# An LSTM and six layers of windowed attention on one core: the layer stage's hardware loops written out

## The reference

```python
def step(carry, xw_t):                      # LSTM, 1024 steps in sequence
    a = xw_t + prev_h @ Wh
    i, f, o, g = sigmoid, sigmoid, sigmoid, tanh of the four parts of a
    next_c = f * prev_c + i * g
    next_h = o * tanh(next_c)
...
for i in range(6):
    x = attn_layer(shift_tokens(x), Wqkv[i], q_scale[i], k_scale[i], Wo[i]) + x   # 16 heads of 64, windows of 64 with one look back
    x = ffn_layer(shift_tokens(x), ln_g[i], ln_b[i], W1[i], b1[i], W2[i], b2[i]) + x
return x_in + x
```

## Time and profile before

| | |
|---|---|
| time, median of 3 runs | 5339.57 us (5339.14 to 5344.78) |
| the profiled execution | 5329.88 us |
| its span, first to last instruction | 5326.9 us |
| busy: TensorE, weight loads | 4817.3 us (90%), 3753.0 us (70%) |
| busy: VectorE, ScalarE, GpSimd | 3541.4, 2630.4, 1899.0 us |
| start of the first slot's scores, start of the last chunk's | 630.39 us, 4857.08 us |
| instructions in the trace | 206473 |

### The profile page before, as it was taken

The page is one execution under the profiler, slowest core; times in us unless marked ns, Lnnn a source line. Parts: engine busy times, 40 slices in busy tenths (PEclk is TensorE's granted clock), DMA queues, the critical chain, the costliest instruction groups (busy, mean ns, idle before and its releaser), DMA issues.

```text
span 5326.9 us, 206473 instructions
## 1 busy us (share of the span) xinstructions
PE 4817.3 (90%) x79632; PEld 3753.0 (70%) x79632; DVE 3541.4 (66%) x14167; ACT 2630.4 (49%) x8193; POOL 1899.0 (36%) x2070
## 2 busy tenths in 40 slices
PE   4665699999999999999999999999999999999888
PEld 1445577777777777777777777777777777776666
DVE  8665566676667667676666666676666666666554
ACT  0112355555555555555555555455455555455554
POOL 3640233333333333333333333333333333334442
PEclk6555699999999999999999999999999999999999
DMA  3020122322322322323322322332332332233431
GB/s 128 2 85 0 45 82 86 107 85 89 105 82 79 119 82 78 106 82 90 107 82 78 119 82 78 104 94 81 104 90 82 106 95 79 89 105 91 120 118 53
DMA packets 311470, 464.73 MB, mean 87 GB/s; under 512 B 213264, under 2 KB 239888, under 8 KB 297616
## 3 DMA queue, kind: packets, MB, share of 16 engines
q1 hardware_dynamic: 310544, 451.92, 28.3%
HBM read 381.93 MB, written 69.93 MB: 85 GB/s over the span
## 4 chain that ended last, share of the span: by engine, by line
PE 59%; issue 12%; DVE 9%; POOL 4%; ACT 3%; ACTq 0%; POOLq 0%; DMA 0%; DVEq 0%; SPq 0%
PE mm L914 12%; PE gates L185 12%; PE st L1026 7%; PE gates L177 5%; PE dd L1026 4%; PE st L953 3%; PE pt L1053 3%; PE pt L1061 3%; PE tt L926 2%; PE pt L967 2%; POOL va L817 2%; PE dd L983 2%; DVE pr L1398 2%; PE st L995 1%; PE st L943 1%
## 5 line engine op out<-in xcount | busy, mean ns | idle before, releaser
L802 POOL TENSOR_TENSOR turned<-raw,rotl 128x256 f32<-128x256 f32 x768 | 716.4, 948 | 1810.6 <-ACT raw L1145 1523.2
L914 PE MATMUL mm<-wqkv,xa 128*128 128x512 f32 x2304 | 1196.6, 632 | 11.1 <-DMA rot<-in_rotary 8.5
L185 PE MATMUL gates<-hp,whp 128*128 128x6 bf16 x28672 | 849.9, 166 | 23.7 <-DVE hp L230 23.4
L185 PEld LDWEIGHTS gates<-hp,whp 128*128 128x128 bf16 x28672 | 784.7, 96 | 59.0 <-DVE hp L230 31.9
L1196 ACT ACTIVATE pr<-st,nb,qn 128x128 f32<-128x128 f32 x1536 | 686.8, 462 | 134.4 <-DVE nb L1386 133.6
L192 ACT ACTIVATE state<-gsum 128x16 f32<-128x16 f32 x896 | 195.1, 218 | 987.2 <-DVE gsum L200 979.1
L914 PEld LDWEIGHTS mm<-wqkv,xa 128*128 128x128 f32 x2304 | 391.3, 196 | 249.3 <-issue 227.5
L177 PEld LDWEIGHTS gates<-hp,whp 128*128 128x128 bf16 x14336 | 425.7, 96 | 149.0 <-issue 91.0
L177 PE MATMUL gates<-hp,whp 128*128 128x2 bf16 x14336 | 485.7, 163 | 27.5 <-DVE hp L215 27.3
L200 DVE TENSOR_REDUCE gsum<-gates 128x16 f32<-128x48 f32 x896 | 182.0, 203 | 489.8 <-PE gates L185 483.2
L810 POOL TENSOR_TENSOR qn<-ss,power 128x8 f32<-128x8 f32 x192 | 321.1, 1672 | 514.5 <-DVE ss L1357 505.3
(11 more groups left out here) (135 smaller groups left out, 9796.9 us busy)
## 6 DMA issues: line engine op xcount, KB each, us to landing
wqkv<-in_Wqkv SPq DMA_DIRECT2D x288, 512.0 KB, 3.9
w<-in_W SPq DMA_DIRECT2D x48, 1364.0 KB, 5.8
wo<-in_Wo SPq DMA_DIRECT2D x48, 1024.0 KB, 5.5
w<-in_W SPq DMA_DIRECT2D x48, 768.0 KB, 4.5
kT<-k_windows SPq DMA_DIRECT2D x96, 256.0 KB, 5.2
va<-v_windows SPq DMA_DIRECT2D x96, 256.0 KB, 5.1
k_windows<-kT SPq DMA_DIRECT2D x96, 256.0 KB, 4.2
v_windows<-vb SPq DMA_DIRECT2D x96, 256.0 KB, 4.5
```

The source lines that it names most:

```text
L185: last = nc.tensor.matmul(g[:, m * PARTS * BATCH:(m + 1) * PARTS * BATCH], self.whp[:, p, k, m * P:(m + 1) * P], self.hp[:, k, :, :].rearr ...
L802: ins = nc.gpsimd.tensor_tensor(dst[:, :, a, :], src[:, :, 1 - a, :], tab[:, :, a, :].broadcast_to([P, 8, HALF]), ALU.mult)
L914: ins = nc.tensor.matmul(mm[c % 2][:, :], shifted(xa, y.b, k), wqkv[:, c, k, :], start=(k == 1), stop=(k == 0))
```

## The change

The `Fori` loops over chunks and layers in the layer stage become Python loops, on all five engines. All 96 slots are written out one after the other in each engine's stream. `c`, `l`, `it` and the step numbers are then Python numbers: every wait compares with a constant and every address is fixed. The order of the instructions in a slot isn't changed. The loop of the first stage stays.

```diff
@@ passes(): TensorE, VectorE, ScalarE, GpSimd
-            with eng.Fori(0, CHUNKS - 1) as c:
-                with eng.Fori(0, DEPTH - 1) as l:
-                    layer(c, l, l + c * DEPTH, True)
-                last_layer(c, c * DEPTH + (DEPTH - 1), True)
-            c = CHUNKS - 1
-            with eng.Fori(0, DEPTH - 1) as l:
-                layer(c, l, l + c * DEPTH, False)
-            last_layer(c, c * DEPTH + (DEPTH - 1), False)
+            for c in range(CHUNKS):
+                recur = c < CHUNKS - 1
+                for l in range(DEPTH - 1):
+                    layer(c, l, c * DEPTH + l, recur)
+                last_layer(c, c * DEPTH + (DEPTH - 1), recur)
```

## The result

The changed kernel takes 5176.9 us in the median of 4 runs (5173.6 to 5177.4), the kernel before 5339.4 us beside it (5329.1 to 5344.8). The ratio is 0.9697, with a 95% interval of 0.968 to 0.9713. The forecast was 5138 us with a range up to 5172; the time is 39 us above the one and 5 us above the other. The profiled execution took 5177.4 us, its span is 5175.6 us.

The account below looks back on a forecast made before the run. TensorE and VectorE waiting for code after taken loop jumps was taken as the bound. Savings of 180 + 21 + 1 = 202 us took the profiled 5329.9 to 5128; with 9.7 carried, 5138 us, range 5097 to 5172.

Parts of the forecast that it names:

- the jumps' missing code: Layer stage: TensorE and VectorE wait for code after 34 taken loop jumps; removing them saves 180 us after corrections.
- The base of the sum: Recurrent layer stage without jumps: 7 chunks x (10 x 48.43 + 47.17 + 45.66) = 4040 us, against 4226.7 in the trace.
- The last chunk: Slots without recurrence: removing jumps saves nothing there, removing registers 0.1 x 10 = 1 us.
- granted clock 1.00 from slot 1 to the end: Sign of being right: TensorE's clock stays full through all slots after the first.
- registers, 0.25 us per slot: Loop waits and addresses become constants in the layer stage: 0.25 us for 84 slots, 21 us saved; range 0 to 0.75.
- the correction for `k` = 0, 5 us: Slots of the first kind may be 0.15 us longer than slot 9; times 35, 5 us less gain.
- the excess behind a jump as "two things": Slots just behind a jump take 50.77 us through VectorE's late start and TensorE's half clock for 4.8 us.
- 9.7 us from the profiled execution to the median: Median of the runs lay 9.7 us over the profiled execution before; carried, it turns 5128 into 5138 us.
- Registers at 1 us per slot: Rival, chance 0.09: register instructions beside the recurrence's waits cost 1 us per slot, giving 5075 us.
- Only the gap goes, 5216: Rival, chance 0.06: only the 3.0 us gap at each of 34 jumps goes, 102 us, with registers 22: 5216 us.
- the trace speaks against the Trainium skill: VectorE's loop body would fit the skill's 512 held instructions, yet 4.6 us pass behind its jump.
- Code streamed as a cost: Rival, chance 0.03: ScalarE, GpSimd and SyncE must fetch straight code, 4.6 us once per slot, 440 us: 5580 us.

Follow-up runs that it names:

- pe_dve: Changed kernel with only TensorE's and VectorE's streams written out, loops and registers kept on the other three engines: 5186.0 us, 0.972 of the kernel before.
- pe_only: Changed kernel with only TensorE's stream written out, loops and registers kept on the other four engines: 5377.9 us, 1.0073 of the kernel before.
- dve_only: Changed kernel with only VectorE's stream written out, loops kept on the other engines: 5328.3 us, 0.9989 of the kernel before.
- fill_end: Changed kernel plus two useless 448-column matmuls per slot, placed near the slot's end: 5179.5 us, 0.9712 of the kernel before.
- fill_mid: Changed kernel plus two useless 448-column matmuls per slot, placed in the second recurrence step: 5212.7 us, 0.9777 of the kernel before.
- pad: Changed kernel with W2's last, 42-row block multiplied with all 128 rows, `u` cleared once: 5076.6 us, 0.9521 of the kernel before.
- before_pad: Kernel before, loops kept, with W2's last, 42-row block multiplied with all 128 rows: 5307.1 us, 0.9948 of the kernel before.
- reg: Changed kernel with a zero register added to `it` and step number, so waits and `hist` addresses are computed in registers: 5188.7 us, 0.9719 of the kernel before.
- pad_reg: Changed kernel with full-height W2 matmuls, plus a zero register added to `it` and step number on every engine: 5086.5 us, 0.9534 of the kernel before.

## Why the prediction missed by 39 us

**Right: the jumps' missing code.** That TensorE's 34 late starts and the half clock behind them would go, worth 5.5 us a jump, is shown by the waits and by pe_dve, which gains nearly all of it, where pe_only and dve_only gain nothing. The base of the sum, slots without a jump, held in form: 48.38 measured for 48.43, 47.07 for 47.17, 45.55 for 45.66 us. The last chunk gave what the registers gave, 38.62 for 38.72. Nothing streamed in cost time. The prediction had a few more packets, and for the whole that was wrong: by the pages of the two profiles the packets of q8 fell from 638 to 597 and those of q14 from 288 to 224, so loops had fetched more, not less; in a stretch of the last chunk 8 came where none had, as said.

**Failed: "granted clock 1.00 from slot 1 to the end".** This is the main step. The sum multiplied a clean slot by 70. In the kernel before, no more than three slots in a row were without a jump, and none of them showed a fall; of 84 in a row about every third shows one. The step that failed is the carrying over of two or three clean slots, with their clock at full, to a stretch of 84, which no row showed. 25 falls x (50.01 - 48.38) = 41 us. The stage adds up with it: 70 x 48.38 + 7 x 47.07 + 7 x 45.56 = 4035 us, the first slot 0.85 us over, and 41 make 4077 (measured 4076.7). The term was absent from the sum and no rival had it. fill_end and fill_mid show that it hangs on TensorE's work at the end of a slot, and pad that it can be had back; with loops, in before_pad, the same edit gave more half clock and not less. Why one boundary in three and not each, though the instructions ahead are the same, stays open; so does whether pad keeps the clock by doing more in its 42-row matmuls or by closing the gaps around them.

**Failed in size: registers, 0.25 us per slot.** Shown: 0.05 us between clean slots before and after, about 0.10 in reg and pad_reg. In the sum it makes 16 us: the undisturbed slots were forecast to 4040 - 21 = 4019 us and came to 4035. `xn` in slot 92, from which the value came, did start earlier, 24.91 us into the slot (5040.57 - 5015.66) for 25.14; but the slot became only 0.10 us shorter. The delay is real on the chain and TensorE has other work meanwhile.

```profile
5040.57 0.55 DVE L1419 TENSOR_SCALAR xn<-st,mv,rsd 128x256 f32<-128x256 f32 x1 [0.67 <-POOL rsd L851]
```

**Unneeded: the correction for `k` = 0, 5 us.** Both kinds take 48.38; the 0.11 us between slots 92 and 93 exists only without the recurrence. The first slot, for which 2 us were left, is 0.85 us over. So, from 4025.7 forecast for the stage: +41 (falls) +16 (registers) -5 (`k` = 0) -1 (first slot) = 4077.

**Wrong reading: the excess behind a jump as "two things".** VectorE's late start had no share of its own. dve_only takes it away and gains 0.1%; and the earlier trace rows already said so: in the slot of 50.77 us TensorE was idle for 0.89 us, in slot 9 for 0.80. The excess was half clock alone. The sum wasn't touched, since both went, but a reader of it would have expected pe_only to be faster, and it is slower: with TensorE's stall gone, VectorE's is what TensorE waits for.

**Carried: 9.7 us from the profiled execution to the median.** Here the profiled execution is 0.5 us over the median. Against the profiled time, 5128 forecast and 5177.4 measured, the miss is 49 us, and the carried term hid 10 of it. The range's high end, 5172, was made of the jumps and registers alone, with the clock at full, and so had no room for the 41 us.

**The rivals.** Registers at 1 us per slot: excluded by reg. Only the gap goes, 5216: excluded, for slots behind a former jump lost their 2.4 us too, and yet the time lies between it and the forecast. That the trace speaks against the Trainium skill, as the prediction had it, was read too strongly. Its section ("Runtime: NRT & Kernel Launch", "Instruction fetch mechanics") gives 512 instructions as two blocks of 256, fetched in sequence, and has a taken branch wait for code when its target isn't in the current two. VectorE's body has 421 instructions in the trace and so spans two or three blocks; its 4.6 us before and its two stalls in pe_only, 4.06 and 2.02 us, don't contradict that. ScalarE's body of 251 goes on 0.2 us after its inner jumps. Where the blocks lie no trace here shows. Code streamed as a cost: on TensorE, VectorE and ScalarE no wait for "issue" as long as 1 us stands in the changed kernel's slots. GpSimd has one of 16.2 us, in slot 13, where it otherwise waits as long for ScalarE; slots 12 and 13 together take 98.3 us, two clean ones and one fall, so it cost nothing.

## What to carry to other kernels

A stall that several engines have at the same jump may have to be taken from all of them at once: here TensorE's alone gave +0.7%, VectorE's alone -0.1%, both -2.8%. A steady state longer than any that the trace shows is an extrapolation; where TensorE is busy nearly all the time and its clock can fall, keep a term for that and look at what TensorE does at the seams of the pattern. And look for the few matmuls of odd height between full ones: making them full-height was worth 100 us here, 1.9% of the time, with one cleared buffer, though a quarter of that with the loops in place.

## What the runs showed of the hardware that I had not expected

- The granted clock fell to 0.50 for 3.4 us in a stream with 840 matmuls per slot and no gap of its own ahead (49.25 us busy of 50.02), 25 times in the stage.
- 42-row matmuls among 128-row ones cost 0.65 us per slot for four of them, and the clock stayed at 1.00 once they were full-height.
- Where TensorE has no stall of its own (pe_only), VectorE waits twice behind its jump for nothing that another engine did, 4.06 us and, some 2 us later in its body, 2.02 us.
- A hint of the jump's target took VectorE's stall away and shortened TensorE's inner branch from 3.8 to 2.0 us, but put a wait of up to 3.9 us on TensorE behind the loop's exit, where no jump is taken, and made the kernel 0.6% slower.
- The same edit (full-height W2) was worth 1.9% without loops and 0.5% with them: in the looped kernel the half clock at the jumps grew from 239 to 314 us and TensorE's gaps from 99.6 to 123.0 us, which took most of it back.
